# Conditioning products of 51 rows on two halves of the array, in place of 128-row products

## The chip, the cores and the metric

The kernel runs on one NeuronCore of a Trainium2 chip. Its engines are TensorE (PE in the profile, with its weight loads as PEld), VectorE (DVE), ScalarE (ACT), GpSimd (POOL) and SyncE (SP), which here only issues DMA transfers. The engines run side by side and meet at semaphores. The metric is the device time of one execution in microseconds (us).

## The reference

Four graph layers run one after another on 625 nodes with 512 features, 20000 edges, each on a layer-normalised input and added to it: a graph convolution, a mean aggregation with a gate, a conditioned attention network of 4 blocks, and a two-direction attention layer. The change lies in the third:

```python
def _cond_layer_norm(x, cond, sw, sb, bw, bb):
    xn = (x - mu) * jax.lax.rsqrt(var + EPS)
    scale = cond @ sw + sb
    bias = cond @ bw + bb
    return xn * (1.0 + scale) + bias

cond = silu(emb @ f_w1 + f_b1) @ f_w2 + f_b2        # [625, 16], once
for i in range(4):
    y = _cond_layer_norm(x, cond, s1_w[i], s1_b[i], b1_w[i], b1_b[i])
    x = x + _sparse_attention(y, ...)
    y = _cond_layer_norm(x, cond, s2_w[i], s2_b[i], b2_w[i], b2_b[i])
    x = x + (relu(y @ m_w1[i] + m_b1[i]) @ m_w2[i] + m_b2[i])
```

`cond` has 16 columns, so `cond @ sw` is a product that contracts 16 values (and 1 + the bias `sb` can ride along as rows of ones).

## The kernel before

The 640 padded nodes are 5 tiles of 128 (`NT = 5`). A row of features has 512 columns, one PSUM bank. Weights and activations are held as a high part, rounded to fp32r, and a low part, the rest; a product of full precision is three fp32r products (high by high, high by low, low by high).

**Conditioning.** For each block, each of its two normalisations (`ln` 0 and 1) and each tile `t`, `pe_cond` (L1655) computes 1 + scale and the offset: two products of 512 columns into the two banks of one of three double-bank buffers (`big`). Both contract 128 rows: `condT` [128, 640] and one of the four operands of `condw` [128, 4, 512] (scale and offset of `ln` 0, scale and offset of `ln` 1). The 128 rows are four blocks of 32: rows 0 to 15 of a block carry `cond` (high in blocks 0 and 2, the rest in 1 and 3) against the weights (high in the lower 64 rows, the rest in the upper 64), row 16 the bias against ones, row 17 the constant 1 or 0. There are 4 x 2 x 5 = 40 pairs.

DVE uses a pair in two steps (L1970 `centred`, L1979 `scaled`), PE turns the result (`turn`, L1641, four transposes), ACT rounds it (L1414) and DVE takes the rest (L1985).

**Order on PE.** It is written out by hand. Second normalisation (`norm_order(1)`, L1757): pair, pair, turn, pair, turn, and so on, with output products (`row_terms`, L1713; twelve of 512 columns per tile) ahead of the pairs of tiles 1 to 3 and part of them ahead of the pair of tile 0. First normalisation: the pairs of tiles 0 and 1 stand together behind the third tile of the previous block's last products (L1788), those of tiles 2 and 3 ahead of the first value product (L1690), that of tile 4 behind it (L1694). In block 0, tiles 0 and 1 stand together (L1945), and tiles 2 and 3 (L1950).

**Filling `condw`.** SP issues, in one fixed queue with all weight transfers, six transfers for each operand into a staging buffer (`stage_cond`, L1153): the 16 weight rows four times, the bias row, the constant row. ACT rounds all 128 rows into `condw` (L1506), POOL writes the rest into the upper 64 (L1332). PE's first pair of a normalisation waits for that (`split_done`, L1659). `condT` is made once: `f_w2` [16, 128] holds `f_w2` four times side by side (L1193), and `pick` and column 2 of `fcol`, from sums over the identity, tell which rows carry what (L2181 to L2187).

The last layer has products of few rows too: `spread` (L741) multiplies a 16-row or 8-row operand, at L743, between products and transposes of 128 rows.

Of the kernel before, what the change touches and what calls it, by code (L numbers as in the profile page):

```python
# [17 lines left out]
P = 128  # L18
# [112 lines left out]
PERBLK = 6 * KT  # L131
F_LOADS = 2 + 2 * 4
VECS = 3 * BLOCKS * KT + 4 * KT + 1
# [22 lines left out]
def build(nc, a, out):  # L156
    ctx = ExitStack()
    with ctx:
# [310 lines left out]
        def ld_count(n):  # L469


            dmas = {S_COND + i: 6 for i in range(4)}
            for b in range(BLOCKS - 1):
                dmas |= {S_BLK + b * S_PERBLK + PERBLK + i: 6 for i in range(4)}
            return sum(16 * dmas.get(i, 1) for i in range(n + 1) if slot(i) == slot(n))
# [641 lines left out]
        def _(sp):  # L1117
# [34 lines left out]

            def stage_cond(n, w, b, extra, it=0):  # L1153


                before = n - (OUTER if slot(n) < OUTER else STAGE)
                sp.wait_ge(split_done, before + 1 + it * S_PERBLK)
                for i in range(4):
                    sp.dma_start(staged[slot(n)][32 * i:32 * i + C16, :], w).then_inc(raw_ld[slot(n)], 16)
                sp.dma_start(staged[slot(n)][C16:P:32, :], b.unsqueeze(0).broadcast_to([4, D])).then_inc(raw_ld[slot(n)], 16)  # L1160
                c = extra.shape[1]
                sp.dma_start(staged[slot(n)][C16 + 1:P:32, :].rearrange("p (k c) -> p k c", c=c),
                             extra[0:4, :].unsqueeze(1).broadcast_to([4, D // c, c])).then_inc(raw_ld[slot(n)], 16)

# [35 lines left out]
            for it in range(BLOCKS):  # L1200


                for i, (w, b, extra) in enumerate(conds):
                    if it == 0 and i == OUTER:
                        sp.wait_ge(big_full, BIG0[f"l1_{NT - 1}"] + 1)
                    stage_cond(S_COND + i, w[it], b[it], extra, it)
                for q in (WV, WQ, WK, WO, W1, W2):
# [70 lines left out]
        def _(g):  # L1278
# [42 lines left out]
            def rest_cond(n, kind, it=0, behind=None):  # L1321


                if behind is None:
                    g.wait_ge(split_done, n + it * S_PERBLK)
                else:
                    g.wait_ge(rstd_up, behind + 1)
                r = staged[slot(n)]
                to = condw[:, kind, :]
# [90 lines left out]

        def act_l2(act, high):
            def turned(ln, t, b):
                act_turned(act, ln, t, b)

            for it in range(BLOCKS):
# [63 lines left out]
                for o in range(KT):  # L1489
# [4 lines left out]
                    for i in ((), (), (0,), (1, 2, 3))[o] if it < BLOCKS - 1 else ():  # L1494
                        high(S_BLK + PERBLK + i, condw[:, i, :], it)
                if it < BLOCKS - 1:
# [5 lines left out]
        def _(act):  # L1502
            def high(n, to, it=0):

                act.wait_ge(raw_ld[slot(n)], ld_count(n) + it * LD_PERBLK)
                act.activation(to, staged[slot(n)], ACT.Copy).then_inc(shi_up, 1)  # L1506


# [76 lines left out]
            for t in range(2, NT):  # L1585
                left_high(t)
                for i in (2 * t - 4, 2 * t - 3) if t < 4 else ():
                    high(S_COND + i, condw[:, i, :])

# [8 lines left out]
            for t in range(NT):  # L1598
# [8 lines left out]
                for i in (2 * t - 4, 2 * t - 3) if t in (2, 3) else ():  # L1607
                    high(S_BLK + WV + i, ringpart(RING_BLK + WV + i)[0])
            act_l2(act, high)
            act_l3(act, high, turned_relu)  # L1610
# [44 lines left out]
        def pe_cond(pe, ln, t, b):  # L1655
# [506 lines left out]
        def _(dve):  # L2162
# [17 lines left out]
            dve.wait_ge(const1, 1)  # L2180
            blocks = ident[:, :].rearrange("p (i n) -> p i n", i=4)  # L2181
            dve.tensor_reduce(pick[:, 0:4], blocks[:, :, C16:C16 + 2], AX.X, ALU.add).then_inc(cb_one, 1)
            dve.wait_ge(cb_one, 1)
            dve.tensor_reduce(fcol[:, 2:3], pick[:, 0:4], AX.X, ALU.add).then_inc(cb_one, 1)
            dve.wait_ge(cb_one, 2)
            step(dve.tensor_reduce(pick[:, 0:4], blocks, AX.X, ALU.add))
            step(dve.tensor_tensor(pick[:, 4:5], pick[:, 1:2], pick[:, 3:4], ALU.add))  # L2187
            dve.wait_ge(e_ld, 16 * 7)
# [324 lines left out]
```

## Time and profile before

| | us |
|---|---|
| median of three runs | 959.19 |
| lowest, highest | 955.20, 959.53 |
| the profiled execution | 958.63 |
| its span in the trace | 956.8 |
| PE busy in the span | 853.3 (89%) |
| DVE busy | 661.0 (69%) |
| POOL busy | 516.9 (54%) |
| ACT busy | 459.0 (48%) |

The span is what the trace covers; 1.8 us lie around it. Matmuls are pipelined, and their recorded durations overlap, so a step of PE is read from start to start, not from the durations. In the chain of waits a piece ends where the next one begins, and the rows there are shifted by the time a product takes to come out.

### The profile page before, as it was taken

How to read it: one execution, taken by the hardware profiler on the slowest of the kernel's cores; microseconds unless marked ns; L12 is line 12 of the kernel's file. 1: busy time of each engine (PE TensorE's matmuls, PEld its weight loads, DVE VectorE, ACT ScalarE, POOL GpSimd, SP SyncE). 2: the span in 40 equal slices, each digit the busy share in tenths (PEclk: the TensorE clock that was granted, in tenths of full speed). 3: DMA queues.
4: the chain of work that ended last, by engine and by line, in shares of the span. 5: the costliest groups of instructions: out<-in, count | busy, mean ns of one | idle time of the engine just before them, and what ended most of it. 6: DMA issues, size and time to landing. Idle time of an engine off the chain costs nothing.

```text
span 956.8 us, 18275 instructions
## 1 busy us (share of the span) xinstructions
PE 853.3 (89%) x6760; PEld 748.8 (78%) x6760; DVE 661.0 (69%) x1305; ACT 459.0 (48%) x764; POOL 516.9 (54%) x601
## 2 busy tenths in 40 slices
PE   3899869989999899999998999989999989888786
PEld 2798757878898787989786989878798978764456
DVE  7999888792565774276667256577427667679896
ACT  5777563234664233376133456323337615245664
POOL 7677624268532565843176753266574319447771
PEclk9999978999999899999999999989999999978998
DMA  5100000133200023300016220003230002100111
GB/s 127 35 0 0 22 23 23 47 99 89 67 1 1 23 82 98 110 23 2 1 40 171 69 66 1 2 23 89 90 113 21 1 1 77 34 1 29 43 56 54
DMA packets 49362, 44.34 MB, mean 46 GB/s; under 512 B 6014, under 2 KB 37154, under 8 KB 49300
## 3 DMA queue, kind: packets, MB, share of 16 engines
q1 hardware_dynamic: 47492, 40.21, 14.8%
q10 hardware_dynamic: 1808, 3.31, 1.6%
q8 instruction: 38, 0.62, 0.3%
q14 instruction: 24, 0.20, 0.1%
HBM read 42.04 MB, written 1.33 MB: 45 GB/s over the span
## 4 chain that ended last, share of the span: by engine, by line
PE 62%; DVE 20%; issue 6%; ACT 5%; POOL 3%; DVEq 2%; DMA 1%; SPq 0%; POOLq 0%
PE psum L1623 25%; PE psum L1617 16%; PE psum L1713 11%; PE psum L1641 5%; DVE arena L2070 2%; ACT arena L1470 2%; DVE arena L919 2%; PE psum L1661 1%; DVE stats L2198 1%; POOL ringw L1319 1%; DVE hot_dst L956 1%; PE psum L841 1%; DVEq L2302 1%; DVE hot_dst L2297 1%; DVE xn L2211 1%
## 5 line engine op out<-in xcount | busy, mean ns | idle before, releaser
L1260 POOL TENSOR_SCALAR acc<-acc,rden,flag 128x640 f32<-128x640 f32 x80 | 70.5, 882 | 110.7 <-DVE rden L2066 110.2
L1713 PE MATMUL psum<-ringw,arena 128*128 128x512 f32 x480 | 118.8, 396 | 3.6 <-DVE arena L2078 2.5
L1623 PE MATMUL psum<-ringw,arena 128*128 128x512 f32 (+1 forms) x418 | 101.3, 395 | 16.6 <-POOL ringw L1319 6.5
L1623 PE MATMUL psum<-arena 128*128 128x384 f32 (+3 forms) x675 | 115.7, 324 | 0.0
L1617 PE MATMUL psum<-arena,ringw 128*128 128x320 f32 x768 | 113.3, 309 | 0.0
L1617 PEld LDWEIGHTS psum<-arena,ringw 128*128 128x128 f32 x768 | 112.9, 188 | 0.3
L1623 PEld LDWEIGHTS psum<-arena 128*128 128x128 f32 x675 | 105.0, 189 | 6.7 <-DVE arena L2070 1.1
L1713 PEld LDWEIGHTS psum<-ringw,arena 128*128 128x128 f32 x480 | 87.8, 188 | 23.7 <-DVE arena L2078 3.5
L1623 PEld LDWEIGHTS psum<-ringw,arena 128*128 128x128 f32 x418 | 76.6, 206 | 33.7 <-issue 14.7
L1641 PE MATMUL psum<-ident,acc 128*128 128x128 f32 x560 | 81.5, 277 | 19.6 <-DVE acc L1979 15.7
L1617 PE MATMUL psum<-arena 128*128 128x320 f32 x480 | 88.5, 322 | 6.2 <-DVE arena L2070 5.6
L1319 POOL TENSOR_TENSOR ringw<-raw,ringw 128x512 fp32r<-128x512 f32 x56 | 72.1, 1295 | 31.8 <-ACT ringw L1506 31.8
L1641 PEld LDWEIGHTS psum<-ident,acc 128*128 128x128 f32 x560 | 66.8, 142 | 28.6 <-DVE acc L1979 18.5
L2050 DVE SCALAR_TENSOR_TENSOR arena<-psum,cols,arena 128x640 fp32r<-128x640 f32 x32 | 28.3, 884 | 87.7 <-ACT arena L1457 87.7
L1312 POOL TENSOR_SCALAR veps<-mv 128x1 f32<-128x1 f32 x60 | 14.4, 240 | 135.1 <-DVE mv L2202 133.9
L1617 PEld LDWEIGHTS psum<-arena 128*128 128x128 f32 x480 | 70.8, 188 | 14.9 <-DVE arena L2070 12.7
L2070 DVE TENSOR_TENSOR arena<-psum,arena 128x640 fp32r<-128x640 f32 x80 | 65.1, 818 | 15.4 <-ACT arena L1470 15.4
L1370 POOL TENSOR_TENSOR hot_dst<-hot_dst,w_part 128x160 bf16<-128x160 bf16 x120 | 58.2, 512 | 27.0 <-DVE hot_dst L2297 27.0
L1319 POOL TENSOR_TENSOR ringw<-xn,ringw 128x512 fp32r<-128x512 f32 x49 | 65.2, 1344 | 13.5 <-ACT ringw L1506 13.5
L1465 ACT ACTIVATE acc<-acc,nsmax 128x640 f32<-128x640 f32 x80 | 66.0, 825 | 9.5 <-DVE nsmax L2061 8.5
L2061 DVE CUSTOM_DVE_ANT_0 acc<-psum,mask 128x640 f32<-128x640 f32 x80 | 64.8, 814 | 0.0
L1414 ACT ACTIVATE arena<-psum 128x512 fp32r<-128x512 f32 x40 | 23.8, 595 | 84.7 <-PE psum L1641 84.6
(283 smaller groups left out, 1874.6 us busy)
## 6 DMA issues: line engine op xcount, KB each, us to landing
raw<-in_L_gnn_m_w SPq DMA_DIRECT2D x16, 256.0 KB
xn<-in_L_gnn_m_w SPq DMA_DIRECT2D x16, 256.0 KB
raw<-in_L_gnn_wv SPq DMA_DIRECT2D x8, 256.0 KB
xn<-in_L_gnn_wv SPq DMA_DIRECT2D x8, 256.0 KB
raw<-in_L_gnn_wq SPq DMA_DIRECT2D x8, 256.0 KB
xn<-in_L_gnn_wq SPq DMA_DIRECT2D x8, 256.0 KB
raw<-in_L_gnn_wk SPq DMA_DIRECT2D x8, 256.0 KB
xn<-in_L_gnn_wk SPq DMA_DIRECT2D x8, 256.0 KB
```

Source lines behind the costliest of these rows:

```text
L1260: g.tensor_scalar(pbuf[:, k % 4, :], pbuf[:, k % 4, :], rden[:, k:k + 1], flag[:, 1, k % NT:k % NT + 1], ALU.mult, ALU.mult).then_inc(pn_u ...
L1319: g.tensor_tensor(to[1], staged[slot(n)], to[0].bitcast(F32), ALU.subtract).then_inc(split_done, 1)
L1370: ins = g.tensor_tensor(hot_dst[:, b, :, (i + 1) * WIN:(i + 2) * WIN], hot, w_part[:, i, :, bass.ds(gr, 1)].broadcast_to([P, CH, WIN]), AL ...
L1414: act.activation(yT[:, 0, :, t * P:(t + 1) * P], bflat(u)[:, 0:D].rearrange("p (k n) -> p k n", k=KT), ACT.Copy).then_inc(yhi_up, 1)
L1465: act.activation(pbuf[:, k % 4, :], pbuf[:, k % 4, :], ACT.Exp, bias=nsmax[:, k:k + 1], scale=-1.0, accum_out=den[:, k:k + 1]).then_inc(ex ...
L1617: ins = pe.matmul(big[buf(u)][:, h, 0:HALF], l, r[:, h * HALF:(h + 1) * HALF], start=(i == 0), stop=(i == len(terms) - 1))
L1623: ins = pe.matmul(to, l, r, start=(i == 0), stop=(i == len(terms) - 1))
L1641: ins = pe.transpose(bflat(u)[:, k * P:(k + 1) * P], src[:, k * P:(k + 1) * P], ident[:, :])
L1713: ins = pe.matmul(brow(ROWBLK[f"{name}{t}"]), l, r, start=(pieces[0] + i == 0), stop=(pieces[-1] == KT - 1 and i == len(terms) - 1))
L2050: dve.scalar_tensor_tensor(wide(to[:, 1, h, :]), bwide(u), bqk[:, i, bass.ds(it * KT + h, 1)], wide(f32(to[:, 0, h, :])), ALU.add, ALU.sub ...
L2061: dve.tensor_tensor_reduce(wide(pbuf[:, k % 4, :]), bwide(u), wide(mask[:, t, :]), -DH ** -0.5, 3e38, ALU.add, ALU.min, nsmax[:, k:k + 1]) ...
L2070: dve.tensor_tensor(pT[:, 1, :, t * P:(t + 1) * P], bflat(u).rearrange("p (k n) -> p k n", k=NT), f32(pT[:, 0, :, t * P:(t + 1) * P]), ALU ...
```

## The change

`condw` becomes [128, 2, 512], one entry for each normalisation. Scale takes rows 0 to 50, offset rows 64 to 114 (`CROWS = 64`, `CK = 51`): 16 weight rows three times (high for `cond` high, high for `cond`'s rest, low for `cond` high; the product of the two low parts is gone), the bias twice (high and rest), the constant once. `condT` is laid out in the same way in both halves. Each product now contracts 51 rows, scale in the lower half of the array and offset in the upper one, still into two banks.

```diff
-F_LOADS = 2 + 2 * 4
+F_LOADS = 2 + 2 * 6
+CROWS = 64
+CLOW, CBIAS, CK = 2 * C16, 3 * C16, 3 * C16 + 3
...
-        condw = sb("condw", [P, 4, D], F32R)
+        condw = sb("condw", [P, 2, D], F32R)
...
-            def stage_cond(n, w, b, extra, it=0):
+            def stage_cond(n, kind, w, b, extra, it=0):
...
-                for i in range(4):
-                    sp.dma_start(staged[slot(n)][32 * i:32 * i + C16, :], w).then_inc(raw_ld[slot(n)], 16)
-                sp.dma_start(staged[slot(n)][C16:P:32, :], b.unsqueeze(0).broadcast_to([4, D])).then_inc(raw_ld[slot(n)], 16)
+                r = staged[slot(n)][CROWS * kind:CROWS * kind + CK, :]
+                for i in range(3):
+                    sp.dma_start(r[C16 * i:C16 * (i + 1), :], w).then_inc(raw_ld[slot(n)], 16)
+                sp.dma_start(r[CBIAS:CBIAS + 2, :], b.unsqueeze(0).broadcast_to([2, D])).then_inc(raw_ld[slot(n)], 16)
...
-            for i in range(4):
-                sp.dma_start(f_w2[:, 32 * i:32 * i + C16], a["L2_gnn_f_w2"]).then_inc(f_ld, 16)
-                sp.dma_start(fcol[32 * i:32 * i + C16, 2:3], a["L2_gnn_f_b2"].unsqueeze(1)).then_inc(f_ld, 16)
+            for lo in range(0, P, CROWS):
+                for i in range(lo, lo + CBIAS, C16):
+                    sp.dma_start(f_w2[:, i:i + C16], a["L2_gnn_f_w2"]).then_inc(f_ld, 16)
+                    sp.dma_start(fcol[i:i + C16, 2:3], a["L2_gnn_f_b2"].unsqueeze(1)).then_inc(f_ld, 16)
...
-                lo = slice(P // 2, P)
+                lo = slice(CROWS * (kind % 2) + CLOW, CROWS * (kind % 2) + CBIAS + 1)
...
+            def high_cond(n, kind, it=0):
+
+                rows = slice(CROWS * (kind % 2), CROWS * (kind % 2) + CK)
+                act.wait_ge(raw_ld[slot(n)], ld_count(n) + it * LD_PERBLK)
+                act.activation(condw[rows, kind // 2, :], staged[slot(n)][rows, :], ACT.Copy).then_inc(shi_up, 1)
...
-                ins = pe.matmul(big[buf(u)][:, i, :], condT[:, t * P:(t + 1) * P], condw[:, 2 * ln + i, :], start=True, stop=True)
+                rows = slice(CROWS * i, CROWS * i + CK)
+                ins = pe.matmul(big[buf(u)][:, i, :], condT[rows, t * P:(t + 1) * P], condw[rows, ln, :], start=True, stop=True)
```

On PE the order of instructions stays. In the second normalisation of block 0 stands, before and after alike but for line numbers (before: L1713 output products, L1661 conditioning pair, L1641 transposes):

```order
L1661 MATMUL psum<-condw,condT 128x512 x2
L1713 MATMUL psum<-ringw,arena 128x512 x12
L1661 MATMUL psum<-condw,condT 128x512 x2
L1641 MATMUL psum<-ident,acc 128x128 x4
L1713 MATMUL psum<-ringw,arena 128x512 x12
```

The listing counts the output's partitions, 128 in both; what has changed is the rows that each pair contracts. SP's queue ahead of block 0, with the transfers for the first operand (`raw` is a staging buffer), before and then after:

```order
L1151 DMA raw<-in_L_gnn_W_r 128x512 x2
L1159 DMA raw<-in_L_gnn_s_w 16x512 x4
L1160 DMA raw<-in_L_gnn_s_b 4x512
L1162 DMA raw<-ones 4x4x128
L1159 DMA raw<-in_L_gnn_b_w 16x512 x4
```

```order
L1155 DMA raw<-in_L_gnn_W_r 128x512 x2
L1164 DMA raw<-in_L_gnn_s_w 16x512 x3
L1165 DMA raw<-in_L_gnn_s_b 2x512
L1167 DMA raw<-ones 1x4x128
L1164 DMA raw<-in_L_gnn_b_w 16x512 x3
```

One transfer of weight rows less for each operand, so all that stands behind it in the queue moves up by one. At the start of the kernel four small transfers more (`f_w2` and `fcol`, twice two) stand in the same queue ahead of the first layer-1 weights.

## Rows read from the trace of the kernel before

**Rows 1.** The page: busy time of each engine, and the chain by engine.
```profile
PE 853.3 (89%) x6760; PEld 748.8 (78%) x6760; DVE 661.0 (69%) x1305; ACT 459.0 (48%) x764; POOL 516.9 (54%) x601
...
PE 62%; DVE 20%; issue 6%; ACT 5%; POOL 3%; DVEq 2%; DMA 1%; SPq 0%; POOLq 0%
```

**Rows 2.** Chain in time, second normalisation, block 0: start us, us, what.
```profile
309.39 0.47 PE psum L1661 x2
...
313.04 0.44 PE psum L1641 x4
...
316.25 0.46 PE psum L1661 x2
...
319.89 0.47 PE psum L1661 x2
```

**Rows 3.** Groups by line: busy us, mean ns, idle before, releaser.
```profile
L1970 DVE SCALAR_TENSOR_TENSOR acc<-z,mv,psum 128x512 f32<-128x512 f32 x40 | 29.8, 745 | 6.1 <-PE psum L1661 5.7
```

**Rows 4.** Chain in time, first normalisation of block 1.
```profile
351.19 0.91 PE psum L1661 x4
...
358.75 2.52 POOL ringw L1319 x2
...
361.41 4.59 PE psum L1623 x12
```

**Rows 5.** Timeline, one pair of block 0: start us, us, engine, line.
```profile
312.19 0.19 PEld L1661 LDWEIGHTS psum<-condw,condT 128*128 128x128 f32 x1
...
312.42 0.62 PE L1661 MATMUL psum<-condw,condT 128*128 128x512 f32 x2
...
312.88 0.27 PE L1641 MATMUL psum<-ident,acc 128*128 128x128 f32 x1
```

**Rows 6.** Timeline, products of 16 rows (L743) among products of 128.
```profile
842.88 0.28 PE L1623 MATMUL psum<-ringw,arena 128*128 128x256 f32 x1
...
843.08 0.29 PEld L743 LDWEIGHTS psum<-arena 16*128 16x128 f32 x2
...
843.09 0.41 PE L743 MATMUL psum<-arena 16*128 16x320 f32 x1
...
843.34 0.30 PE L743 MATMUL psum<-arena 16*128 16x320 f32 x1
...
843.57 0.33 PE L761 MATMUL psum<-ident,mask 128*128 128x128 f32 x1
...
843.74 0.38 PE L761 MATMUL psum<-ident,mask 128*128 128x128 f32 x2
```

**Rows 7.** Chain in time: long runs of 320 columns and of 256.
```profile
223.15 28.17 PE psum L1617 x192
...
841.73 1.43 PE psum L1623 x12
```

**Rows 8.** Timeline, a pair behind a wait; in brackets idle and releaser.
```profile
359.38 0.50 PE L1661 MATMUL psum<-condw,condT 128*128 128x512 f32 x1 [0.48 <-DVE arena L1985]
...
359.72 0.40 PE L1661 MATMUL psum<-condw,condT 128*128 128x512 f32 x1
```

**Rows 9.** Timeline, filling `condw` for block 1: SP's issue and POOL.
```profile
337.75 1.73 SPq L1159 DMA_DIRECT2D raw<-in_L_gnn_s_w  x4
...
346.20 1.29 POOL L1332 TENSOR_TENSOR condw<-raw,condw 64x512 fp32r<-64x512 f32 x1 [1.88 <-ACT condw L1506]
```

**Rows 10.** Timeline, start: last small load, its user, ACT at layer-1 weights.
```profile
15.22 0.42 SPq L1194 DMA_DIRECT2D fcol<-in_L_gnn_f_b  x1
...
28.81 0.71 PE L1842 MATMUL psum<-mask,f_w 64*16 64x320 f32 x2
...
30.98 1.14 ACT L1506 ACTIVATE ringw<-raw 128x512 fp32r<-128x512 f32 x2
```

**Rows 11.** Windows: us, PE busy, granted clock, DMA share, GB/s.
```profile
361.40:366.00 4.60, 4.59 (x14) 0.63 0.71 146
516.00:519.00 3.00, 3.00 (x14) 1.00 0.92 117
671.60:676.30 4.70, 4.66 (x15) 0.64 0.55 174
```

More of the change, by code:

```diff
@@ L469, in ld_count @@
         def ld_count(n):
-            dmas = {S_COND + i: 6 for i in range(4)}
+            dmas = {S_COND + i: 5 for i in range(4)}
             for b in range(BLOCKS - 1):
-                dmas |= {S_BLK + b * S_PERBLK + PERBLK + i: 6 for i in range(4)}
+                dmas |= {S_BLK + b * S_PERBLK + PERBLK + i: 5 for i in range(4)}
             return sum(16 * dmas.get(i, 1) for i in range(n + 1) if slot(i) == slot(n))
@@ L1205, in _ @@
                         sp.wait_ge(big_full, BIG0[f"l1_{NT - 1}"] + 1)
-                    stage_cond(S_COND + i, w[it], b[it], extra, it)
+                    stage_cond(S_COND + i, i % 2, w[it], b[it], extra, it)
                 for q in (WV, WQ, WK, WO, W1, W2):
@@ L1328, in rest_cond @@
                 r = staged[slot(n)]
-                to = condw[:, kind, :]
+                to = condw[:, kind // 2, :]
                 g.wait_ge(shi_up, n + 1 + it * S_PERBLK)
-                lo = slice(P // 2, P)
+                lo = slice(CROWS * (kind % 2) + CLOW, CROWS * (kind % 2) + CBIAS + 1)
                 g.tensor_tensor(to[lo, :], r[lo, :], to[lo, :].bitcast(F32), ALU.subtract).then_inc(split_done, 1)
@@ L1419, in act_bias, with act_l2 @@
                 act.dma_start(bias[:, i, :], a["L2_gnn_" + b][it].partition_broadcast(P)).then_inc(bias_ld, 16)
-        def act_l2(act, high):
+        def act_l2(act, high, high_cond):
             def turned(ln, t, b):
@@ L1494, in act_l2 @@
                     for i in ((), (), (0,), (1, 2, 3))[o] if it < BLOCKS - 1 else ():
-                        high(S_BLK + PERBLK + i, condw[:, i, :], it)
+                        high_cond(S_BLK + PERBLK + i, i, it)
                 if it < BLOCKS - 1:
@@ L1587, in _ @@
                 for i in (2 * t - 4, 2 * t - 3) if t < 4 else ():
-                    high(S_COND + i, condw[:, i, :])
+                    high_cond(S_COND + i, i)
             def gate(t):
@@ L1608, in _ @@
                     high(S_BLK + WV + i, ringpart(RING_BLK + WV + i)[0])
-            act_l2(act, high)
+            act_l2(act, high, high_cond)
             act_l3(act, high, turned_relu)
@@ L2180, in _ @@
             dve.wait_ge(const1, 1)
-            blocks = ident[:, :].rearrange("p (i n) -> p i n", i=4)
-            dve.tensor_reduce(pick[:, 0:4], blocks[:, :, C16:C16 + 2], AX.X, ALU.add).then_inc(cb_one, 1)
+            halves = ident[:, :].rearrange("p (i n) -> p i n", i=2)
+            dve.tensor_reduce(pick[:, 0:2], halves[:, :, CBIAS:CK], AX.X, ALU.add).then_inc(cb_one, 1)
             dve.wait_ge(cb_one, 1)
-            dve.tensor_reduce(fcol[:, 2:3], pick[:, 0:4], AX.X, ALU.add).then_inc(cb_one, 1)
+            dve.tensor_tensor(fcol[:, 2:3], pick[:, 0:1], pick[:, 1:2], ALU.add).then_inc(cb_one, 1)
             dve.wait_ge(cb_one, 2)
-            step(dve.tensor_reduce(pick[:, 0:4], blocks, AX.X, ALU.add))
-            step(dve.tensor_tensor(pick[:, 4:5], pick[:, 1:2], pick[:, 3:4], ALU.add))
+            step(dve.tensor_reduce(pick[:, 0:2], halves[:, :, C16:CLOW], AX.X, ALU.add))
+            step(dve.tensor_tensor(pick[:, 4:5], pick[:, 0:1], pick[:, 1:2], ALU.add))
             dve.wait_ge(e_ld, 16 * 7)
```

4 lines of the change are left out of this document (2 added, 2 removed).

## Prediction

> **What bounds the kernel now.** I read the shares of the chain of waits first [rows 1]: TensorE (PE) makes up 62% of the chain that ended last, VectorE (DVE) 20%, and a PE that is busy 89% of the span is not saturated by that alone, so the question is whether PE is the chain at the places that the change touches. The chain in order of time answers it. In the second normalisation of block 0 [rows 2] it runs PE, PE, PE from 309.39 to 320.4 us: a conditioning pair (0.46 to 0.47 us), twelve output products, four transposes (0.44 us), and again, 3.64 us from the third pair (316.25) to the fourth (319.89). Behind the fourth pair the chain goes over to DVE. DVE is near but not on it: the grouped row of L1970 shows 40 executions with 6.1 us of idle time before them, 5.7 of it waiting for these same products [rows 3]. So each ns that a pair takes is paid there, as long as DVE keeps this slack.
>
> The chain names the pairs 24 times: 16 singles in the second normalisation (4 in each of 4 blocks; the fourth of each block is the one after which DVE takes over), 3 singles in the first normalisation of blocks 1 to 3 (tile 4), and 5 doubles, two pairs back to back (two in the entry of block 0, one before each of blocks 1 to 3). Two singles and a double are in [rows 2, 4]. That is 19 x 0.46 + 5 x 0.91 = 13.3 us and 29 of the 40 pairs. The other 11 (tile 4 of the second norm, tiles 2 and 3 of the first in blocks 1 to 3, tile 4 in block 0) lie in PE's waits.
>
> **The change, part 1: the products.** Count (80), columns (512), order and waits stay; each product now contracts 51 rows, in rows 0 to 50 or 64 to 114, so each is laid out for half an array. What a pair costs now: 0.46 us from the first start to the next instruction's (312.42 to 312.88), 0.23 each, with the weight load of the first started at 312.19, 0.23 us ahead, under the product before it [rows 5]. The best that two halves can give is both products in 0.23 us, 0.23 saved.
>
> But the same trace shows what a product of another row count costs among full ones. L743 contracts 16 or 8 rows, 320 columns, between 128-row products [rows 6]. Steady spacings: 0.119 us for 256 columns (1.43/12), 0.147 for 320 (28.17/192) [rows 7], 0.11 for a transpose (0.44/4) [rows 2], 0.23 for 512 [rows 5]. Against these:
> - the last full product before L743: 842.88 to 843.09, 0.21 against 0.12, **+0.09**. L743's load starts at 843.08, not ahead.
> - the first L743 product: 843.09 to 843.34, 0.25 against 0.15, **+0.10**: a load that nothing covers. A second reading of that price: after a wait, the pair at 359.38 has its second product at 359.72, 0.34 against 0.23, +0.11 [rows 8]. I take 0.11.
> - the second L743 product to the next full one: 843.34 to 843.57, 0.23 against 0.15, **+0.09**.
> - the first full one after it: 843.57 to 843.74, 0.17 against 0.11, **+0.06** before a transpose. Before a product I take **+0.11**, the uncovered load again.
>
> This is not a change of data type: 842.88 and 843.09 are the same type, and fp32 transposes beside fp32r products of 128 rows (312.88) show nothing of it. So changing the row grouping drains PE and uncovers a load, going in and coming out: 0.35 to 0.40 us an island.
>
> TensorEngine Tiling (the Trainium skill, Key Properties) says that changing the tiling mode drains the engine, while a change of tile within one mode does not. By it the 51-row pair pays the same toll as L743, at 64 rows as at 32; the trace agrees for L743 with its 0.09 us on either side.
>
> Inside the island nothing in the trace shows two halves at work. Bounds: the loads can follow one another (0.11 each, as 843.08 and the next) with the products overlapping; the loads can overlap too; or the products can queue at 0.23. I take the first, since the nearest row, L743's two loads in 0.29 us with 0.18 each [rows 6], shows loads spaced by 0.11, and two products in different rows into different banks share neither weights nor output.
> - single pair, product behind it: 0.09 + 0.11 + 0.11 + 0.23 + 0.09 + 0.11 = 0.74 against 0.46, **+0.28**, x7 (the first of the second norm in 4 blocks, 3 in the first norm): +1.96
> - single, transposes behind it: 0.69, **+0.23**, x8: +1.84
> - the fourth, where the chain leaves with the product's end: 0.09 + 0.11 + 0.11 + 0.23 = 0.54, **+0.08**, x4: +0.32
> - double: 0.09 + 4 x 0.11 + 0.23 + 0.09 + 0.11 = 0.96 against 0.91, **+0.05**, x5: +0.25
>
> Sum **+4.4 us**. With the loads overlapping (0.11 less per single; a double 0.09 + 0.11 + 0.46 + 0.20 = 0.86, -0.05): 8 x 0.12 + 7 x 0.17 - 4 x 0.03 - 5 x 0.05 = **+1.8**. With the products queued (0.12 more per single; a double 1.32, +0.41): 8 x 0.35 + 7 x 0.40 + 4 x 0.20 + 5 x 0.41 = **+8.5**. Of the 11 pairs off the chain ten stand ahead of a PE wait that is longer than the toll (0.48 us ahead of 359.38 [rows 8]); the eleventh, in block 0, lies where the chain runs through DVE and ACT. Without that cover they would add at most 11 x 0.28 = 3 us.
>
> **Part 2: filling the weights.** ScalarE (ACT) and GpSimd (POOL) keep their 16 instructions each on `condw`, with 51 rows for 128 and 17 for 64. Durations go by columns as far as rows show: POOL takes 1.29 us on 64x512 here [rows 9] and 2.52/2 = 1.26 on each 128x512 of L1319 [rows 4]. So nothing. SyncE issues 5 transfers instead of 6 for each of 16 operands: 0.43 us less a time (1.73/4). ACT does wait for these transfers, but the products don't: POOL has the first two done at 346.20 + 1.29 = 347.5, and PE uses them at 351.19 [rows 4, 9]. Gain on the chain 0; if it were on it, 4 x 0.43 = 1.7 a block. What comes earlier are the value weights behind them in SyncE's queue, whose products wait for POOL's L1319 [rows 4], which waits for ACT work that waits for PE.
>
> **Part 3: the start.** Four more small loads of `f_w2` and `fcol`, 0.42 us each in SyncE's queue, +1.7 us behind 15.22, ahead of the layer-1 weights [rows 10]. Their user on PE starts at 28.81, 13 us after the last issue; the layer-1 weights are first read by ACT at 30.98. Hidden; if not, at most 1.7. DVE's three small sums over `ident` shrink before its own wait for the edge list. 0.
>
> **Against the time.** The profiled execution took 958.63 us, its span 956.8, 1.8 around it; +4.4 makes the span 961.2. The three timed runs have the median 959.19 (955.20 to 959.53), so the forecast is 959.2 + 4.4 = **963.6 us**.
>
> **Rivals.**
> - *No toll, halves overlap* (the gain that the halves promise). The toll was read at 8 and 16 rows; at 64 it might not exist. Then 19 x -0.23 + 5 x -0.45 = -6.6: **952.6 us**. For it: 51 rows on two halves fill almost the array. Against it: 842.88 to 843.09 is a toll between full rows and a part, and nothing in it depends on how many rows the part has. TensorEngine Tiling (the Trainium skill, Theoretical Speedup) allows up to 2x for a contraction of 64 or less, which is this case. 0.18.
> - *Loads overlap too*: +1.8, **961.0 us**. For it: the halves share no weights. Against it: loads spaced by 0.11 in [rows 6], though in the same rows. TensorE: Matmul & The Clock Gate (the Trainium skill, Part 3) has products of different row tiles starting some 4 ns apart; by that it is this case. 0.20.
> - *Products queue*: toll and no overlap, the slower end: +8.5, **967.7 us**. It decides where the second product of a pair starts 0.23 us or more behind the first. No row excludes it. 0.14.
> - *The clock after the pairs decides.* In blocks 1 to 3 PE waits for POOL before the first value product, and those twelve products took 4.59 us [rows 4] at a mean granted clock of 0.63 (in part the 1.2 GHz level) in block 1, but 3.00 us at 1.00 in block 2 [rows 11]; block 3 was like block 1. Two of three were slow in this execution; all quick is -3.2, all slow +1.6, so 956 to 960.8 us without any net effect of the pairs. 0.10, and it blurs all others by 2 us.
> - The forecast: 0.38.
>
> **How the numbers follow.** A comparison of this kernel can tell about 0.5% from no change, 954.4 to 964.0 us. The forecast lies just inside, so with the clock's 2 us I give 0.16 of its 0.38 to slower. Slower: 0.16 + 0.13 (queued) + 0.03 = 0.32. Faster: 0.12 of the no-toll case, 0.01 of the clock's: 0.13. Within: 0.55. Range 953.5 to 968.5: the bounds 952.6 and 967.7 with the clock's share, about 0.15 left out on both sides together.
>
> **What the changed profile would show.** Products of the pair with 51 rows; the one before them followed by a gap of 0.32 us instead of 0.23; their first load no longer 0.23 us ahead; the second product 0.1 us behind the first (0.00: loads overlap; 0.23 or more: queued; 0.23 with the load ahead: no toll). The step from pair to pair in the second norm 3.9 us instead of 3.65. L1970's idle before it grows by the same. I am wrong if the load stays ahead, or if DVE or POOL turns out to set that step.

## The result, and the profile after

| | before | after |
|---|---|---|
| median of 11 runs each | 958.67 us (953.78 to 961.80) | 962.22 us (960.74 to 964.56) |
| ratio after/before, 95% interval | | 1.0047 (1.0032 to 1.0063) |
| span of the profiled execution | 956.8 us | 960.0 us |

The interval lies at +3.1 to +6.0 us, just around the 0.5% that a measurement of this kernel can tell from no change. Forecast were 963.6 us, and "within 0.5%" as the likeliest case. The sections below show that the number came out nearly right although one term of the sum was wrong: the pairs of products cost about half of what was forecast, and TensorE's clock, which the forecast had put at nothing net, goes with the rest.

The page of the changed kernel, busy time and chain, against [rows 1]:

```profile
PE 855.9 (89%) x6760; PEld 740.6 (77%) x6760; DVE 661.8 (69%) x1305; ACT 459.2 (48%) x764; POOL 515.8 (54%) x601
...
PE 62%; DVE 20%; ACT 6%; issue 5%; POOL 3%; DVEq 2%; DMA 1%; SPq 0%; ACTq 0%
```

The bound is the same: PE is still 62% of the chain. The chain in order of time, second normalisation of block 0, against [rows 2] (L1674 is now the conditioning pair, L1653 the transposes, L1726 the output products):

```profile
312.56 0.42 PE psum L1674 x2
312.98 2.98 PE psum L1726 x12
315.97 0.43 PE psum L1674 x2
316.40 0.59 PE psum L1653 x4
316.99 2.75 PE psum L1726 x12
319.74 0.43 PE psum L1674 x2
```

From pair to pair it is 3.77 us (315.97 to 319.74) where it was 3.64. The pair itself is a little shorter (0.43 for 0.46), but the four transposes behind it take 0.59 instead of 0.44. Behind the first pair the twelve products take 2.98, where the kernel before has this row:

```profile
309.86 2.72 PE psum L1713 x12
```

From the first pair to the second it is 3.41 us (312.56 to 315.97) where it was 3.19.

One pair in the timeline, loads (PEld) and products (PE), against [rows 5] (start us, us, engine, line, rows contracted, in brackets idle time before it):

```profile
319.35 0.39 PE L1726 MATMUL psum<-ringw,arena 128*128 128x512 f32 x1
...
319.67 0.19 PEld L1674 LDWEIGHTS psum<-condw,condT 51*128 51x128 f32 x2 [0.35 <-issue]
...
319.67 0.50 PE L1674 MATMUL psum<-condw,condT 51*128 51x512 f32 x2
...
320.10 0.33 PE L1653 MATMUL psum<-ident,acc 128*128 128x128 f32 x1
```

Read it against the forecast. The product before the pair keeps PE for 0.32 us (319.35 to 319.67) instead of 0.23, and no load runs ahead: the load engine is idle for 0.35 us. That is the toll of 0.09 us that L743 had shown [rows 6]. But *two* loads fit in 0.19 us, and *two* products in 0.50. By form, one load lasts 183 ns and one product 482 on average, so loads and products of the two halves run side by side; in the trace each starts 3 ns behind its partner. 0.43 us later (320.10) the first transpose follows.

```profile
L1983 DVE SCALAR_TENSOR_TENSOR acc<-z,mv,psum 128x512 f32<-128x512 f32 x40 | 29.7, 744 | 7.8 <-PE psum L1674 7.4
...
L1674 PE MATMUL psum<-condw,condT 51*128 51x512 f32 x80 | 18.6, 482 | 1.6 <-DVE arena L1998 1.6
...
L1674 PEld LDWEIGHTS psum<-condw,condT 51*128 51x128 f32 x80 | 7.1, 183 | 11.8 <-issue 9.3 <-DVE arena L1998 2.5
```

These are rows of the groups by line and form (busy us, mean ns, idle before). VectorE's wait before L1970, 6.1 us in [rows 3], is 7.8 us now, and the part of it that ends with a pair went from 5.7 to 7.4: 1.7 us more. These waits lie at the 16 single pairs of the second normalisations, so this is a second reading of what those 16 cost.

TensorEngine Tiling (the Trainium skill, Key Properties) has a change of tiling mode drain the engine; the trace agrees, with 0.09 us on the way in. TensorE: Matmul & The Clock Gate (the Trainium skill, Part 3) has products of different row tiles starting some 4 ns apart; the trace agrees, with 3 ns.

**The pairs, place by place.** From these starts, the cost of a pair up to the instruction after the next, in the changed kernel less the kernel before:
- single, transposes behind it: +0.09 (entry), -0.03 (0.43 for 0.46), +0.06 (next load uncovered): **+0.12**, 8 times
- single, product behind it: the same with +0.11 for the load behind it: **+0.17**, 7 times
- fourth pair, behind which the chain goes over to VectorE: **-0.02**, 4 times
- double: **-0.04 to -0.07**, 5 times; its row is 0.66 us where [rows 4] has 0.91

Sum: 8 x 0.12 + 7 x 0.17 - 4 x 0.02 - 5 x 0.05 = **+1.8 us**. It is a little low: the step from the first pair of a second normalisation to the second grew by 0.22 us here, not by 0.17. The profiled spans differ by 3.2 and the ratio says 4.5. So something else adds 1.4 to 2.7 us, and the experiments had to find it.

**Where else the two traces part.** Against the changed kernel they part at two more places, both in the first 210 us. (Later the changed kernel also gains: from the last pair to the end it takes some 168.5 us instead of 170.6, at a mean granted clock of 0.93 instead of 0.92.) The twelve value products of block 0, with PE's wait for GpSimd ahead of them, in the kernel before and then after:

```profile
205.52 3.01 PE L1623 MATMUL psum<-ringw,arena 128*128 128x512 f32 x12 [2.63 <-POOL ringw L1319]
```

```profile
207.10 4.18 PE L1635 MATMUL psum<-ringw,arena 128*128 128x512 f32 x12 [2.69 <-POOL ringw L1325]
```

The wait is the same, but the products take 3.01 us in one and 4.18 in the other. The windows of that stretch (start:end, length, busy time of PE, PEld, DVE, ACT and POOL, then PE's granted clock, DMA share, GB/s), before and after:

```profile
208.00:212.00 4.00, 4.00 (x21) 3.26 (x20) 2.71 (x5) 2.46 (x4) 0.79 (x2) 1.00 0.81 227
```

```profile
208.00:212.00 4.00, 4.00 (x14) 2.92 (x12) 3.10 (x6) 0.81 (x1) 1.65 (x4) 0.57 1.00 261
```

Behind the wait the changed kernel was granted 0.57, most of it the 1.2 GHz level, and the kernel before 1.00. The same happened in the prelude. Chain in time, before and after:

```profile
151.94 2.76 PE psum L1623 x12
...
181.75 0.91 PE psum L1661 x4
```

```profile
151.62 3.89 PE psum L1635 x12
...
183.35 0.66 PE psum L1674 x4
```

Twelve products at 152 us take 3.89 us instead of 2.76, and the first conditioning pair comes 1.6 us later, before any product of 51 rows has run. The mean granted clock up to the first pair is 0.93 in both kernels, so the difference is not how much of the lower level there was but what it fell on: from 145 to 150 us and from 150 to 155 us the kernel before was granted 0.52 and 1.00, the changed kernel 1.00 and 0.66, and the second stretch holds the twelve products.

### The profile page after: what moved, and what is told of

Read it like the earlier page. It is cut to its first block, busy times and chain, and to the rows that moved or that the text cites. A ratio compares the mean times of both kernels' runs of the same rounds, so it can differ in the third digit from the quotient of the medians.

```text
span 960.0 us, 18263 instructions
## 1 busy us (share of the span) xinstructions
PE 855.9 (89%) x6760; PEld 740.6 (77%) x6760; DVE 661.8 (69%) x1305; ACT 459.2 (48%) x764; POOL 515.8 (54%) x601
## 4 chain that ended last, share of the span: by engine, by line
PE 62%; DVE 20%; ACT 6%; issue 5%; POOL 3%; DVEq 2%; DMA 1%; SPq 0%; ACTq 0%
PE psum L1635 24%; PE psum L1629 16%; PE psum L1726 11%; PE psum L1653 5%; DVE arena L2083 2%; ACT arena L1476 2%; DVE arena L923 2%; DVE stats L2211 1%; PE psum L1674 1%; DVE hot_dst L960 1%; PE psum L845 1%; DVEq L2315 1%; POOL ringw L1325 1%; PE psum L1879 1%; DMA bias<-in_L_gnn_m_b 1%
## 5 line engine op out<-in xcount | busy, mean ns | idle before, releaser
L1726 PE MATMUL psum<-ringw,arena 128*128 128x512 f32 x480 | 119.7, 398 | 3.8 <-DVE arena L2091 2.5
L1726 PEld LDWEIGHTS psum<-ringw,arena 128*128 128x128 f32 x480 | 87.3, 188 | 25.6 <-DVE arena L2091 3.5
L1635 PEld LDWEIGHTS psum<-ringw,arena 128*128 128x128 f32 x418 | 77.4, 207 | 34.9 <-issue 16.4
L1653 PE MATMUL psum<-ident,acc 128*128 128x128 f32 x560 | 82.8, 280 | 18.8 <-DVE acc L1992 14.9
L1653 PEld LDWEIGHTS psum<-ident,acc 128*128 128x128 f32 x560 | 66.4, 143 | 28.9 <-DVE acc L1992 17.3
```

Source lines behind the costliest of these rows:

```text
L1635: ins = pe.matmul(to, l, r, start=(i == 0), stop=(i == len(terms) - 1))
L1653: ins = pe.transpose(bflat(u)[:, k * P:(k + 1) * P], src[:, k * P:(k + 1) * P], ident[:, :])
L1726: ins = pe.matmul(brow(ROWBLK[f"{name}{t}"]), l, r, start=(pieces[0] + i == 0), stop=(pieces[-1] == KT - 1 and i == len(terms) - 1))
```

## Experiments

Ratios are against the kernel before, timed beside it on the same chip.

### e1: the products alone

```diff
             for i in range(2):
-                ins = pe.matmul(big[buf(u)][:, i, :], condT[:, t * P:(t + 1) * P], condw[:, 2 * ln + i, :], ...)
+                rows = slice(64 * i, 64 * i + 51)
+                ins = pe.matmul(big[buf(u)][:, i, :], condT[rows, t * P:(t + 1) * P], condw[rows, 2 * ln + i, :], ...)
```

> The kernel before with the products of a conditioning pair cut to 51 rows each, rows 0 to 50 and 64 to 114; the weights' layout, their loads and the start are those of before, so each product leaves out part of its terms. In the changed kernel's trace a pair on the chain costs +0.12 us with transposes behind it, +0.17 with a product behind it, -0.04 as a double, +1.8 us in all, while the medians differ by +3.5 and the spans by +3.2. Theory A (the pairs cost 1.8 and the rest belongs to the start, the loads or the filling of the weights): +1.8 us here, about 960.5, within 0.3 of it in the sum read from the trace. Theory B (everything comes from the pairs, for instance because products of 51 rows make the granted clock fall in places where it did not before): +3.5 to +4.5 here. Theory C (the rest is the scatter of the clock from one execution to the next): +1.8 here and nothing in the run with the filling alone. In the trace: step from pair to pair in the second norm 3.77 us, second product 0.003 us behind the first, gap ahead of the pair 0.32.

Measured: 960.47 us (956.00 to 965.63, 12 runs) against 958.69; ratio 1.0025 (1.0005 to 1.0045). The pairs look as in the changed kernel, 3.77 us from pair to pair:

```profile
314.23 0.43 PE psum L1662 x2
314.66 0.59 PE psum L1641 x4
315.25 2.75 PE psum L1714 x12
318.00 0.43 PE psum L1662 x2
```

+1.8 us in the medians, which is the sum from the rows; the ratio, which weighs the runs otherwise, says 2.4. Theory B (everything comes from the pairs) isn't excluded by the interval, but its point value is missed.

### e2: the filling and the start alone

```diff
-                ins = pe.matmul(big[buf(u)][:, i, :], condT[rows, t * P:(t + 1) * P], condw[rows, ln, :], ...)
+                ins = pe.matmul(big[buf(u)][:, i, :], condT[:, t * P:(t + 1) * P], condw[:, ln, :], ...)
```

(against the changed kernel; ScalarE's copies write 64 rows instead of 51, so that all rows are filled)

> The changed kernel with its start, loads and filling of the weights, but with both products of a pair over all 128 rows as before, so each sums scale and offset (the result differs, the work of TensorE is that of before). Theory A (the rest of the difference belongs to the start, the loads or the filling): +1.7 to +2.7 us against before. Theories B and C (all from the pairs, or scatter of the clock): 0, within 1 us. In the trace the pairs must look as before: load 0.23 us ahead, 0.23 from product to product, 3.64 us from pair to pair in the second norm.

Measured: 958.74 us (12 runs); ratio 1.0008 (0.9990 to 1.0026). The pairs are those of before (0.46 us, 3.65 from one to the next). Theory A, which gave the filling or the start 1.7 to 2.7 us, loses its point value. The parts together give 1.0033, the whole 1.0047; the intervals allow both "it adds up" and a rest of 1 to 2 us. The trace says more than the median: this kernel, too, has the slow twelve products of block 0, without a single product of 51 rows.

```profile
206.99 4.32 PE L1635 MATMUL psum<-ringw,arena 128*128 128x512 f32 x12 [2.64 <-POOL ringw L1325]
```

In return its blocks 1 and 2 ran quick. So the low clock at this one place doesn't need products of 51 rows. How much of it a kernel gets in all is another question; the last part of this section comes back to it.

### e3: both products in the same rows

```diff
+                rows = slice(0, 51)
```

(in e1's place)

> The kernel before with both products of a pair over the same rows 0 to 50 (each leaves out part of its terms). If the two products of the changed kernel run side by side because they lie in different rows, they must now queue: second product 0.23 us or more behind the first. With the toll of 0.09 on either side and uncovered loads as in the trace of after: a single costs 0.32 + 0.23 + 0.43 and so some 0.2 to 0.3 us more than in the changed kernel, doubles 0.35 to 0.45 more, +7 to +9 us against before (about 966 to 968). If the overlap does not hang on the rows (two banks are enough), the pair looks as in the changed kernel, 0.003 us apart, and the time is +1.8.

Measured: 967.45 us (6 runs); ratio 1.0092 (1.0072 to 1.0112), +8.8 us. Its pair, loads and products:

```profile
317.87 0.29 PEld L1662 LDWEIGHTS psum<-condw,condT 51*128 51x128 f32 x2 [0.35 <-issue]
...
317.87 0.73 PE L1662 MATMUL psum<-condw,condT 51*128 51x512 f32 x2
...
318.21 0.39 PE L1662 MATMUL psum<-condw,condT 51*128 51x512 f32 x1
...
318.53 0.33 PE L1641 MATMUL psum<-ident,acc 128*128 128x128 f32 x1
```

The two loads now take 0.29 us (0.11 apart), and the second product starts 0.34 behind the first. The toll on the way in and out is the same as in the changed kernel. So the overlap hangs on the rows and not on the two banks, and this is the "queued" rival, at its price: +8.8 where +8.5 was forecast for it. (The time holds a share of the clock as well, as the end of this section shows.) It also shows why [rows 6] misled: L743's two loads lie in the same rows, as here.

### e4: the changed kernel again

> The changed kernel once more, on the chip of the next two. With the products alone at 51 rows the difference was +1.8 us and with the filling alone +0.05, but the first comparison of the changed kernel gave +3.5. If the rest was the scatter of the clock (in the two profiles the changed kernel met the lower clock at two places in the first 210 us where the kernel before did not, +1.6 us each): +1.8 us against before here, 0.5 to 3. If the two parts need each other for the rest: +3 to +4.5 again.

Measured: 962.04 us (6 runs) against 957.44; ratio 1.0052 (1.0033 to 1.0070). Its trace has the same two low stretches as the first one, with the same lengths to 0.1 us. So the 1.4 to 2.7 us are no chance of one execution (the medians differ by 4.6 us here, the spans by 4.1): the theory of mere scatter from one execution to the next falls, at least in its simple form.

### e5 and e6: each pair four times

```diff
-            for i in range(2):
+            for i in (0, 1) * 4:
```

(e5 in the changed kernel, e6 in the kernel before)

> The changed kernel with each conditioning pair issued four times in a row into the same banks (same result), so an island of eight products of 51 rows. In e1 the step from the first pair of a double to the second is 0.335 us, which is 0.11 + 0.227. Theory A (only the first load of an island is uncovered; the loads of the next pair start 0.105 us after the first, ahead of their products): each further pair costs 0.23 us, so +3 x 0.23 x 29 pairs on the chain = +20 us over the changed kernel, up to +28 where the 11 pairs off the chain are not covered: 982 to 990. Theory B (every pair pays its load, 0.335): +29 to +40, 991 to 1002.

> The kernel before with each conditioning pair issued four times in a row (same result): +3 x 0.454 x 29 = +39.5 us, up to +54 with the 11 others: 998 to 1013. By the theory that a run of halves pays its toll once and then brings two products in 0.23 us, this kernel is slower than the one with eight products of 51 rows by 3 x 0.227 x 29 = 20 us less the toll's 1.8, so 15 to 25 us; if every pair pays its load, by 3 x 0.12 x 29 = 10 less 1.8, so 6 to 11 us.

Measured: halves 975.76 us, ratio 1.0200 (1.0178 to 1.0222); full 992.15 us, ratio 1.0375 (1.0351 to 1.0398). The islands of eight products in the chain, e5 and then e6:

```profile
315.72 1.13 PE psum L1674 x8
316.85 0.59 PE psum L1653 x4
317.43 2.76 PE psum L1726 x12
```

```profile
312.42 1.82 PE psum L1661 x8
314.24 2.72 PE psum L1713 x12
```

And e5's loads and products in the timeline:

```profile
320.12 0.77 PEld L1674 LDWEIGHTS psum<-condw,condT 51*128 51x128 f32 x8 [0.35 <-issue]
...
320.13 1.20 PE L1674 MATMUL psum<-condw,condT 51*128 51x512 f32 x8
```

Three further pairs add 0.70 us (1.13 - 0.43), 0.23 each, against 0.45 each with full rows: inside an island of halves the next loads run ahead again, and only the first is uncovered. The halves do bring two products in the time of one, and with four pairs to an island they save 16.4 us (15 to 25 expected). Both times lie 6 us below what was expected for them alone. The traces show two reasons and don't part them: the repeated pairs fill PE's waits (1.3 us ahead of the first value products of blocks 1 to 3 in the kernel before, none in e6; 1.5 us in the changed kernel, 0.85 in e5), and the value products of all four blocks ran at the higher clock in both. The mean granted clock of their runs was 0.967 and 0.972 (medians), against 0.963 for the kernel before, so part of the 16.4 us may be the clock's.

### e7 and e8: the length of the start

e7 is the changed kernel with the copies of `f_w2` made by one transfer for each half; e8 is the kernel before with four more small transfers.

```diff
-                    sp.dma_start(f_w2[:, i:i + C16], a["L2_gnn_f_w2"]).then_inc(f_ld, 16)
+                sp.dma_start(f_w2[:, lo:lo + CBIAS].rearrange("p (k c) -> p k c", c=C16),
+                             a["L2_gnn_f_w2"].unsqueeze(1).broadcast_to([C16, 3, C16])).then_inc(f_ld, 16)
...
+                sp.dma_start(fcol[C16 + C16 * i:2 * C16 + C16 * i, 3:4], a["L2_gnn_f_b2"].unsqueeze(1)).then_inc(f_ld, 16)
```

> The changed kernel with the six small loads of f_w2 made by two transfers (three copies each), so that SyncE issues as many loads ahead of the layer-1 weights as in the kernel before (same result). In two profiles of the changed kernel and in the one with the filling alone, all with the longer start, the first conditioning pair starts at 182.8 to 183.3 us, with the lower clock in the twelve products from about 150 us; in four profiles with the old start (before, e1, e3, e6) it starts at 179.9 to 181.6. Theory A (the four extra loads shift the work of the prelude against the clock): about 181.5 for the first pair here, and 1.5 to 2 us less than the changed kernel, 960 to 960.5, as in e1. Theory B (the filling's shorter transfers or ScalarE's and VectorE's part set it) : 182.8 to 183.3 and 962 us as before.

> The kernel before with four more small loads (columns of fcol that nothing reads) in SyncE's queue ahead of the layer-1 weights, the number that the change adds; same result. Theory A (the extra loads set the clock's phase in the prelude): first pair at 182.8 to 183.3 instead of 181.4, +1.5 to +2 us. Theory B (they are covered, SyncE waits anyway): nothing, within 0.5 us; then the rest of the changed kernel's loss is not the start.

Measured: e7 963.14 us, ratio 1.0067 (1.0044 to 1.0091); e8 957.15 us, ratio 1.0014 (0.9997 to 1.0030). The double that opens the conditioning in the two chains:

```profile
181.23 0.66 PE psum L1675 x4
```

```profile
182.92 0.91 PE psum L1662 x4
```

Both traces do what theory A says: with the short start the changed kernel has its first pair at 181.2 us instead of 183.3, and with the long start the kernel before has it at 182.9 instead of 181.7. But the time of e7 didn't follow: theory A wanted 960 to 960.5 us, and it stayed at 963. e8 has +1.2 us in the medians with 1.5 to 2 forecast, and its interval holds no change. So the start moves the place of the low clock in the trace, and no change of the time can be told from it.

### e9 to e12: filler products in PE's waits

If the rest is the clock behind PE's waits, then a PE that has something to do there should keep it. The fillers write to a bank that the next real product starts anew.

```diff
                     free_row(pe, u, nr)
+                    for _ in range((4 if it else 10) if t == 0 else 0):
+                        pe.matmul(brow(u)[:, :], condT[:, 0:P], condT[:, 0:D], start=True, stop=True)
                     pe.wait_ge(big_read, BIGBLK[f"t0_{t}"] + nb + 1)
```

(`values`, e9 in the kernel before, e10 in the changed one; e11 and e12 add 8, 4, 1 and 3 of them ahead of four waits at 135 to 151 us)

> The kernel before with filler products into the bank of the first value tile, ahead of TensorE's wait for GpSimd's weights: ten (512 columns, 0.23 us each) in block 0, where it waits 2.63 us, and four in blocks 1 to 3, where it waits 1.29 us. The first real product starts the bank anew, so the result is the same. Stages from the entry pair of a block to the third pair of its first norm take 13.1 us or 14.7 in block 0, and with the stretch ahead 43.3 to 46.0 us in blocks 1 to 3, longer where the twelve value products behind the wait run at the lower clock (3.0 us or 4.6). Theory A (an engine that stays busy keeps the 2.4 GHz through these waits): 13.1 in block 0, about 43 us in all of blocks 1 to 3, so -2.7 us in blocks 1 and 3: 952 to 954 us, ratio 0.994. Theory B (the clock falls there whatever the engine does): no gain, or +0.1 to +0.5 where fillers are late.

> The changed kernel with the same filler products. If the rest of its loss (4.6 us less the 1.8 of the pairs) lies in places where the clock fell in it and not in the kernel before (the entry stage 14.7 for 13.1 us, the prelude 183.1 for 181.4), the fillers take back the entry's 1.6 besides the 2.7 us each in two of the blocks: 955 to 957 us, and the difference to the run with fillers before it shrinks from 4.6 us to 1.8 for the pairs and up to 1.5 for the prelude: 1.8 to 3.3. If the loss is tied to the pairs in another way, the difference between the two stays 4.6.

> The kernel before with the fillers of e9 and 16 more in the prelude's waits: eight ahead of the first product behind the 3.92 us wait (its end was at 140.97 us), four, one and three ahead of the transposes that wait at 144 to 151 us. Same result. If busy work keeps the clock there too, the first conditioning pair starts at 180 to 181 us instead of 181.5 and the time is 0 to 1.5 us below e9: 953.5 to 955.5, ratio 0.9975 to 0.999. If fillers come late and delay the chain, above e9.

> The changed kernel with the same fillers. With those of e10 its first pair stood at 182.9 us against 181.5 in e9, and the two differed by 3.3 us. Theory A (what is left above the pairs' 1.8 is the place where the clock falls in the prelude): the first pair starts within 0.3 us of that of e11, and the difference of the two kernels is 1.8 to 2.4 us. Theory B (there is a cost of the change that no clock explains): it stays 3 us or more, though the prelude is equal.

| | full rows | halves | difference of medians |
|---|---|---|---|
| as they are (e4) | 957.44 us | 962.04 us, 1.0052 (1.0033 to 1.0070) | 4.6 us |
| fillers in the blocks | 955.31 us, 0.9991 (0.9978 to 1.0004) | 958.63 us, 1.0025 (1.0011 to 1.0038) | 3.3 us |
| and in the prelude | 956.89 us, 0.9999 (0.9989 to 1.0010) | 959.10 us, 1.0017 (1.0002 to 1.0032) | 2.2 us |

The block's fillers and the twelve products behind them, in e10:

```profile
203.85 2.43 PE L1697 MATMUL psum<-condT 128*128 128x512 f32 x10
206.77 3.01 PE L1635 MATMUL psum<-ringw,arena 128*128 128x512 f32 x12 [0.49 <-POOL ringw L1325]
```

The wait is 0.49 us instead of 2.69, and the products take 3.01 instead of 4.18. The first conditioning double in e11 and in e12:

```profile
182.09 0.91 PE psum L1661 x4
```

```profile
181.70 0.66 PE psum L1674 x4
```

With fillers in the prelude too, the two kernels reach it at about the same time (181.9 and 181.6 for the first product's own start), and what is left between them is 2.2 us in the medians and 2.1 in the spans (956.0 - 953.9). Against their forecasts, e12 came as its theory A has it (first pairs within 0.3 us, 1.8 to 2.4 between the kernels). e10's difference of 3.3 lies at the edge of its 1.8 to 3.3, but its time missed 955 to 957. e9 (952 to 954 us, ratio 0.994) and e11 (953.5 to 955.5, 0.9975 to 0.999) missed too: in the kernel before the fillers won 1.0 and 0.3 us in the medians, nothing that can be told from no change.

The spans fall like the medians, 4.1, 3.3 and 2.1 us in the three rows; the intervals, some 0.1 to 0.2% wide to either side, would not by themselves separate one row from the next. The same is seen when all profiles are cut at the pairs' starts (us; "entry" from the second double to tile 4's pair in block 0, "blocks" from the last pair of one block to tile 4's pair of the next, "end" from the last pair on, "rest" all that is left, with the second normalisations):

| | to first pair | entry | blocks 1, 2, 3 | end | rest | span |
|---|---|---|---|---|---|---|
| before | 181.6 | 13.1 | 45.6, 43.3, 46.0 | 170.6 | 456.6 | 956.8 |
| e2, filling alone | 183.1 | 14.7 | 43.0, 43.0, 46.0 | 170.4 | 457.0 | 957.1 |
| e8, long start | 182.8 | 14.7 | 46.1, 43.3, 43.3 | 171.7 | 456.8 | 958.6 |
| e9, fillers | 181.7 | 13.2 | 43.3, 43.3, 43.3 | 172.8 | 456.1 | 953.7 |
| e11, more fillers | 181.9 | 13.2 | 44.3, 43.3, 43.2 | 169.6 | 458.4 | 953.9 |
| after | 183.3 | 14.7 | 45.8, 43.0, 45.6 | 168.5 | 459.0 | 960.0 |
| e4, after again | 183.2 | 14.7 | 45.7, 42.9, 45.6 | 169.5 | 459.3 | 960.9 |
| e7, short start | 181.2 | 14.7 | 45.7, 42.9, 46.0 | 170.9 | 458.5 | 959.8 |
| e1, halves alone | 181.6 | 14.7 | 44.8, 45.8, 43.1 | 169.6 | 458.3 | 957.9 |
| e10, fillers | 182.9 | 13.2 | 43.2, 42.9, 44.2 | 170.2 | 460.5 | 957.0 |
| e12, more fillers | 181.6 | 13.2 | 43.6, 43.1, 44.3 | 170.1 | 460.1 | 956.0 |

The entry is 13.1 or 14.7, never between. A block is 44.8 to 46.1 us where its first value products ran in part at the lower level. Where they ran at the higher one it is 43, or 43.6 to 44.3 where another stretch of it was low (e11's block 1 has a mean granted clock of 0.92, its block 2 has 0.96). In all four kernels with fillers the value products of all four blocks took 3.0 us at a granted clock of 1.00, so filler products in the wait do keep the clock for the products behind it; e10, e11 and e12 still have one or two longer blocks each. The rest column holds the single pairs on the chain: its mean is 457.0 over the five profiles with full rows and 459.3 over the six with halves, +2.3 us. Cut in this way, the 3.2 us between the first two profiles are +1.7 to the first pair, +1.6 in the entry, -0.5 in the blocks, -2.1 in the end and +2.4 in the rest. The +2.3 is near the rows' +1.8 (+2.1 for the single pairs), given that the five with full rows differ among themselves by up to 2.3.

**What the clock of all runs says.** One profile shows one execution; every timed run has a mean granted clock of its own. Their medians:

| | runs | mean granted clock |
|---|---|---|
| kernel before (five sets), e2, e8 | 120 | 0.963 to 0.965 |
| changed kernel, e4, e7, e1, e3: products of 51 rows | 41 | 0.9585 to 0.9595 |
| e9, e11: fillers, full rows | 24 | 0.967 |
| e10, e12: fillers, halves | 23 | 0.965, 0.967 |

Every kernel whose pairs contract 51 rows was granted less, with the new filling and the long start (the changed kernel) or without either (e1, e3). The filling and the start with full rows (e2) and the long start alone (e8) were not. With fillers the gap nearly closes, as the times do. A gap of 0.0046 between the pooled means is 4.4 us of the span. Within the sets, a run that was granted less by 1 us of its span was 0.3 us longer, so an estimate for the gap is 1.4 us, of the 1.4 to 2.7 that were to be found. This is a comparison over runs and no experiment on the clock. The first two profiles don't show it: the profiled run of the kernel before had 0.960, below the median of its kind, and that of the changed kernel 0.961.

What stays open: why a kernel with pairs of 51 rows is granted less. It isn't the four extra loads: e8 has them and is not granted less, e1, e3 and e7 have none and are. What the loads seem to move is the prelude. Of the six profiles with the long start and no fillers ahead of the first pair (e5 is one; e3, e5 and e6 are not in the table), five have it at 182.8 to 183.3 us and e5 has it at 181.8; the six with the short start have it at 180.1 to 181.7. But the time of e7 didn't follow. Also, among the profiles without fillers or repeated pairs only the kernel before has an entry of 13.1 us (seven others, e2 and e8 with full rows among them, have 14.7), and there is one profile of it, so the 1.6 us of the entry may be the luck of that execution.

Of the 5.0 us that e9 wins in blocks 1 and 3, the span shows 3.1 and the median 1.0. The end of the kernel gave 2.2 back (172.8 for 170.6) with no edit there, and it goes with the clock: its mean from the last pair on is 0.89 in e9, 0.92 in the kernel before and 0.93 in the changed one, for 172.8, 170.6 and 168.5 us. So in this execution part of what was won at the waits was lost later. None of the versions is faster than the kernel before by more than can be measured; e9, the best, has a ratio of 0.9991 with an interval that holds 1.

## Why the prediction came out as it did

- **What bounds the kernel.** Right. PE is the chain at the pairs, and VectorE's wait at the 16 pairs of the second normalisations grew by 1.7 us.
- **The toll.** Right to the hundredth: 0.32 us ahead of the pair instead of 0.23, no load ahead, 0.06 us more before a transpose, 0.11 before a product. It was read at 16 rows and holds at 51. The rival without a toll, at 952.6 us, is out; it is the one that would have made the change worth making.
- **Inside the pair.** Wrong, and this is the step that failed: "the loads can follow one another (0.11 each, as 843.08 and the next) with the products overlapping", of which I said "I take the first". The second load's term, 0.11 us, measured 0.003. The sum for the pairs is +1.8 (+2.3 in the cut of all profiles), as in the rival "loads overlap too", and not +4.4. The argument against that rival had its weak point in its own words: the loads of [rows 6] are spaced by 0.11 "though in the same rows". e3 shows that in the same rows they are spaced so, and only there.
- **The other pairs off the chain.** Nothing in the traces speaks against their cover: PE's wait ahead of the pair that follows tile 2's is still there.
- **The filling.** Costed at nothing: e2 gives 1.0008 (0.9990 to 1.0026), no effect that can be measured.
- **The start.** Costed at nothing, with 1.7 us at most. The median of e8 (+1.2 us, ratio from 0.9997) can't tell. It does move the work of the prelude against the clock in the trace.
- **The clock.** Named as a rival with 2 us of blur, but only for blocks 1 to 3. In the profiles it decided at the entry of block 0 and in the prelude as well, 1.6 to 1.7 us each, and against the changed kernel both times, while the blocks and the end gave 2.6 us back. Its price there was overrated too: by "all quick is -3.2", e9, whose three blocks were all quick, should have won that much, and its median fell by 1.0. What the forecast lacked is a clock that is lower on average with products of 51 rows (0.959 for 0.964). That goes with the time above the pairs' cost, and with fillers 4.6 us of difference shrink to 2.2. Why it is lower is open.

So 963.6 against 962.2 measured is a near hit with luck in it, made of two errors that cancel: some 2 to 2.6 us too much in the pairs, and some 1.5 to 2.5 us too little for the clock.

## What to carry to other kernels

Splitting an array into halves pays for runs of such products, not for single pairs among full ones: getting in and out costs 0.35 to 0.40 us here (0.09 of drain and an uncovered load each way), and a pair saves 0.23. Take the price of a load or a product from a row with the same placement in the array; a row of another placement gives the toll but not the overlap. And before a difference of 0.3% is put down to an edit, compare the stages behind PE's waits in both traces: a stage that comes in two lengths tells of the clock. Compare the mean clock of all runs as well; two profiles can miss a difference that forty runs show.

## What the runs showed of the hardware

- Two loads into different halves of the array start 3 ns apart and both take 183 ns; two products of 512 columns behind them start 3 ns apart as well. In the same half the loads are 0.11 us apart and the products 0.34 for the first two, 0.23 further on.
- The uncovered load is paid once an island: inside a run of halves, later loads run ahead of their products again (0.23 us for each further pair).
- Behind a wait of 2.6 us twelve products took 3.0 us at the higher level or 4.2 to 4.6 us in part at the lower one. It was the same in two profiles of one kernel, and different in kernels that differ only in small transfers some 190 us earlier. Ten filler products in that wait, and four in the waits of 1.3 to 1.5 us of blocks 1 to 3, brought it to 3.0 us in all 16 places of the four kernels that had them.
- Without fillers, four kernels with pairs of 51 rows had a mean granted clock of 0.959 over 41 runs, three with full rows 0.964 over 120. What ties the two is not shown.
